# Loading x in four strided pieces, spaced over the score sets, instead of one 1 MB transfer

## The reference

```python
B, F, E = 2048, 200, 64                       # r_feature (B, F, E), weight (F, E, E), float32
bilinear = einsum('bie,ied->bid', feature, weight)
out      = einsum('bid,bjd->bij', bilinear, feature)   # (2048, 200, 200)
```

## Time and profile before

| what | value |
|---|---|
| median of 3 runs | 1367.65 us (1362.97 to 1375.2) |
| the profiled execution's own time | 1377.25 us, its span 1375.5 us |
| PE busy | 1213.2 us (88%) |
| DVE, ACT, POOL busy | 1028.0, 1042.1 and 375.3 us |
| bytes moved by DMA | 439.68 MB, mean 320 GB/s |

### The profile page before, as it was taken

The page is one execution under the profiler, slowest core; times in us unless marked ns, Lnnn a source line. Parts: engine busy times, 40 slices in busy tenths (PEclk is TensorE's granted clock), DMA queues, the critical chain, the costliest instruction groups (busy, mean ns, idle before and its releaser), DMA issues.

```text
span 1375.5 us, 57357 instructions
## 1 busy us (share of the span) xinstructions
PE 1213.2 (88%) x24384; PEld 1032.7 (75%) x24384; DVE 1028.0 (75%) x2308; ACT 1042.1 (76%) x1297; POOL 375.3 (27%) x647
## 2 busy tenths in 40 slices
PE   5998998989889898998989989898898988988986
PEld 5787777877779777887778967787677886777853
DVE  1577886777778777787778867787777776777996
ACT  4877887877778776787877968777787877877964
POOL 2222222322223222232222322222232232222322
PEclk8999999999999999999999999999999999999999
DMA  9698998989989899898989989899898998989888
GB/s 259 198 354 315 351 323 316 335 299 335 332 314 350 290 334 352 298 337 303 361 322 332 334 288 349 317 340 320 310 342 301 334 338 286 327 309 342 311 322 310
DMA packets 163821, 439.68 MB, mean 320 GB/s; under 512 B 49904, under 2 KB 49904, under 8 KB 151280
## 3 DMA queue, kind: packets, MB, share of 16 engines
q1 hardware_dynamic: 123632, 317.90, 61.1%
q0 software_dynamic: 39936, 118.12, 28.2%
HBM read 108.13 MB, written 327.68 MB: 317 GB/s over the span
## 4 chain that ended last, share of the span: by engine, by line
PE 54%; DMA 20%; DVE 9%; ACT 6%; issue 6%; SPq 3%; ACTq 0%; POOLq 0%; POOL 0%
PE ps L372 36%; DMA out_dram<-staging 19%; PE ps L340 10%; PE ps L355 9%; ACT staging L401 4%; DVE staging L401 3%; SPq L270 3%; DVE win L452 3%; ACT bl L423 2%; DMA x<-feature_dram 2%; DVE win L459 2%; DVE win L460 1%; DVE win L451 1%; ACT xt L411 0%; ACTq L400 0%
## 5 line engine op out<-in xcount | busy, mean ns | idle before, releaser
L372 PE MATMUL ps<-win,bl 64*64 64x200 f32 x16384 | 848.8, 341 | 87.5 <-ACT staging L401 45.4
L401 ACT COPY staging<-ps 128x800 f32<-128x800 f32 x768 | 613.3, 858 | 264.1 <-PE ps L372 108.0
L372 PEld LDWEIGHTS ps<-win,bl 64*64 64x64 f32 x16384 | 670.6, 177 | 187.5 <-issue 93.6
L313 POOL DMA_DIRECT2D out_dram<-staging x512 | 293.4, 577 | 915.7 <-DVE staging L401 607.4
L401 DVE COPY staging<-ps 128x800 f32<-128x800 f32 x256 | 253.1, 988 | 221.0 <-PE ps L372 220.4
L423 ACT COPY bl<-ps 128x1024 f32<-128x1024 f32 (+2 forms) x320 | 285.2, 920 | 16.0 <-PE ps L355 15.9
L452 DVE COPY win<-xt 128x400 f32<-128x400 f32 x512 | 290.0, 566 | 6.9
L355 PE MATMUL ps<-xt,w 64*64 64x128 f32 x6400 | 248.0, 278 | 46.6 <-ACT staging L401 26.8
L355 PEld LDWEIGHTS ps<-xt,w 64*64 64x64 f32 x6400 | 204.7, 135 | 73.6 <-issue 67.0
L411 ACT COPY xt<-ps 128x1024 f32<-128x1024 f32 (+1 forms) x208 | 211.9, 1019 | 43.2 <-PE ps L340 41.8
L340 PE MATMUL ps<-ident,x 128*128 128x128 f32 x1600 | 227.2, 286 | 18.5 <-DMA x<-feature_dram 14.5
(11 more groups left out here) (4 smaller groups left out, 0.4 us busy)
## 6 DMA issues: line engine op xcount, KB each, us to landing
out_dram<-staging SPq DMA_DIRECT2D x768, 400.0 KB, 5.9
x<-feature_dram POOLq DMA_DIRECT2D x96, 1024.0 KB, 9.5
out_dram<-staging POOLq DMA_DIRECT2D x512, 25.0 KB, 5.0
x<-feature_dram POOLq DMA_DIRECT2D x16, 224.0 KB, 5.9
w<-weight_dram SPq DMA_DIRECT2D x12, 256.0 KB, 11.0
x<-feature_dram POOLq DMA_DIRECT2D x16, 32.0 KB, 5.6
w<-weight_dram SPq DMA_DIRECT2D x1, 64.0 KB, 5.8
w<-weight_dram SPq DMA_DIRECT2D x1, 48.0 KB, 4.5
```

Source lines behind the costliest of these rows:

```text
L313: nc.gpsimd.dma_start(out_v[98 * g:98 * g + 2, OCT * q:OCT * q + OCT, :], staging[64 * g + SPARE[0]:64 * g + SPARE[1] + 1:4, slot].rearran ...
L372: last = nc.tensor.matmul(tile[64 * g:64 * g + 64, r, at:at + F], rows_of_bl(n, r, g, i, s), win[64 * r:64 * r + 64, q % WSLOTS, 2 * (s % ...
L401: copy(staging[:, slot, s % OCT], tile_of("s", n, s)[:, :, 0:2 * F]).then_inc(staged, 1)
```

## The change

Each 1 MB load becomes four of 256 KB. Piece k takes the partitions k, k + 4, k + 8, ... (32 of them, 8 KB each). In the steady state the pieces of one load are assigned to positions in POOL's program that are two sets apart: the first stands one set behind the one at which the 1 MB load stood, the others at 3, 5 and 7 sets behind it. For the load that becomes free with u = 12 (set 51) all four stand another four sets later (56, 58, 60, 62). Every piece has the same wait on `transposed` ahead of it as the load had, and PE waits for all four pieces of a slot. The 224 KB and 32 KB loads stay whole. Ahead of the first block the four pieces of a load follow each other directly.

```diff
+    PIECES = 4
+    APART = 2
...
+    def pieces_of_load(at):
+        return PIECES if at % NX < NX - 1 else 1
...
+    loads_after = defaultdict(list)
+    for n in range(BLOCKS):
+        for s, u in transposed_at.items():
+            at = (n + 1) * NX + u // 2 + XSLOTS
+            if (u % 2 or u == NG - 1) and at < BLOCKS * NX:
+                for piece in range(pieces_of_load(at)):
+                    loads_after[n * SETS + s + 1 + 2 * APART * (u == NG - 1) + APART * piece].append((at, piece))
...
-            def load_x(at):
+            def load_x(at, piece):
...
-                nc.gpsimd.dma_start(x[:, at % XSLOTS, 0:size], rows[:, first + E:first + E + size]
+                batches = slice(piece, NB, pieces_of_load(at))
+                nc.gpsimd.dma_start(x[batches, at % XSLOTS, 0:size], rows[batches, first + E:first + E + size]
                                     ).then_inc(x_loaded[at % XSLOTS], 16)
...
-                    if s in transposed_at and (transposed_at[s] % 2 or transposed_at[s] == NG - 1):
-                        at = (n + 1) * NX + transposed_at[s] // 2 + XSLOTS
-                        if at < BLOCKS * NX:
-                            load_x(at)
+            for s in range(BLOCKS * SETS):
+                if (s + 1) % OCT == 0:
+                    store_rest(s // OCT)
+                for at, piece in loads_after[s]:
+                    load_x(at, piece)
...
-                pe.wait_ge(x_loaded[at % XSLOTS], 16 * (at // XSLOTS + 1))
+                pe.wait_ge(x_loaded[at % XSLOTS], 16 * sum(map(pieces_of_load, range(at % XSLOTS, at + 1, XSLOTS))))
```

More of the change, by code:

```diff
@@ L1 @@
+from collections import defaultdict
 from contextlib import ExitStack
@@ L296, in load_x @@
                     nc.gpsimd.dma_start(x[:, at % XSLOTS, size:size + E], rows[:, 0:E]).then_inc(wrap_loaded, 16)
-            for u in range(XSLOTS):
-                load_x(u)
+            for at in range(XSLOTS):
+                for piece in range(pieces_of_load(at)):
+                    load_x(at, piece)
             nc.gpsimd.memset(ident[:], 0.0).then_inc(ident_zero, 1)
@@ L316, in store_rest @@
                                         ).then_inc(rest_written[slot], 16)
[L318 to L323, removed]
-                    if s in transposed_at and (transposed_at[s] % 2 or transposed_at[s] == NG - 1):
-                        at = (n + 1) * NX + transposed_at[s] // 2 + XSLOTS
-                        if at < BLOCKS * NX:
-                            load_x(at)
+            for at in range(XSLOTS, NX + XSLOTS):
+                for piece in range(pieces_of_load(at)):
+                    load_x(at, piece)
+            for s in range(BLOCKS * SETS):
+                if (s + 1) % OCT == 0:
+                    store_rest(s // OCT)
+                for at, piece in loads_after[s]:
+                    load_x(at, piece)
         @block.tensor
```

## The result

The changed kernel takes 1442.69 us (median of four runs, 1431.02 to 1453.36), the kernel before 1369.39 us in the runs beside it: a ratio of 1.051, 95% interval 1.042 to 1.060. It is slower, as forecast, but by 73 us and not by 27.

The account below looks back on a forecast made before the run. No engine was full; late output stores made ACT wait 104.1 us for staging slots. Block end -45, middle +69 and start +3 sum to +27 us: 1395 us from a median of 1367.65, range 1315 to 1445.

Parts of the forecast that it names:

- The end of the block: Loads behind groups 11 and 12 spread over groups 11 to 14: set 60's wait shrinks, -45 us over 14 blocks.
- Rival C: Block end: pieces hold group 12's stores as long as whole loads, so no gain there; 1440 us, chance 0.08.
- Ahead of the first block: Before the first block each load's last piece is issued 1.7 us later: 0 to 5 us, taken as +3 us.
- The place of the last piece: Mid-block: last piece, behind rest stores, makes PE wait 6.28 us a block at u = 4, 6, 8, 10; net +69 us.
- rival A: Mid-block pieces land quickly, so the kernel is faster: 1343 us at 5.0 us landing, 1311 at 4.0; chance 0.32.
- The sign named for this term: Mid-block: PE's total wait for loads of x rises from 14.5 us to 70 to 95 us, most at u = 4.
- Not all of it is new time: Behind u = 4, 6 and 8, stores catch up while PE waits; staging-slot waits fall away, returning 1.68 us a block.

Follow-up runs that it names:

- e2: Changed kernel, but only the two loads at the end of a block are split and spaced, all others whole and where they were: 1320.04 us, 0.963 of the kernel before.
- e5: Changed kernel plus sixteen identity transposes on PE ahead of the wait for x at u = 4, 6 and 8: 1405.21 us, 1.028 of the kernel before.

## Why the prediction was right and wrong

**The end of the block: right.** -45 us was forecast, -49.6 measured, and e2 shows it alone with -50.9 in the block ends. The mechanism is the one forecast: in the 14 blocks the third store of group 12 lands in 7.9 us on average (11.2 before, 8.0 taken), and ACT idles 2.0 us before set 60 (4.7 before, 2.1 forecast). Rival C, that the end keeps its wait, did not happen.

**Ahead of the first block: right**, +3 forecast, +2.9 measured.

**The place of the last piece: right, its price a little too high.** PE waits at u = 4, 6, 8 and 10 for a piece that POOL issues behind the rest stores of groups 2, 4, 6 and 8. The price of the waits was 6.28 us a block, 94 in all, and is 5.06, 76 in all: a piece landed in 5.7 us and not 5.9, and POOL issued it 0.57 us behind the second rest store and not 0.82 (in block 4 the two rest stores take from 429.30 to 430.45, and the pieces begin at 430.44, half of that behind the second). With 6.38, 6.21 and 6.30 us after that store at u = 4, 6 and 8 the piece came close to the 6.27 at which rival A was to take over: with 76 us in place of 94 the forecast's sum is +9 us, within one per cent. The sign named for this term was off: PE's wait for x was to rise to the order of 70 to 95 us, which is the lengthening of the path, and rose to 152.6, since the new wait also took the place of other idle time and of slower matmuls in the same stretches.

**The step that failed** is the one that began "Not all of it is new time". The slot waits behind u = 4, 6 and 8 did fall away as it says: at full clock, in e5, the stretches add up to 188.2 us, 22.7 less than before, where 15 x 1.68 = 25 was forecast. But it priced PE's work behind a wait at the clock it had before the wait, and so put the clock at nothing without a reason. 26 of 45 times the clock was lower, and 22.7 us of gain became 19.3 us of loss: 42 us that the sum did not have. They make the difference between the forecast of 27 and the 54 us of the profiled execution: 42 from the clock, 2.5 from slot waits that came back a little less, less 18 by which the waits were smaller and 4.6 by which the end gained more, and the 5 us between the stretches. Without the 42 us the parts come to 12 us, less than one per cent: most of the slowdown came from a term that the forecast did not have, and in so far its sign is luck. Some of the loss stays without the falls, as e5 shows, which has its own transposes to pay and is 2.8% above the kernel before.

The Trainium skill (TensorE: Matmul & The Clock Gate, "HAM oscillation — how this bites in real kernels") tells of a kernel in which each DMA wait lets the clock fall and the work after the wait starts slowly, again at every tile. The traces agree in part: the clock was lower in 26 of 45 stretches, with rows at 0.56 to 0.74, and stayed full in the other 19. The kernel before had its own sign of it: at the end of block 0, where set 60 waits, the stretch from set 48 to the next set 0 stands at a granted clock of 0.86, and at the end of block 14, where it doesn't, at 1.00. The row of block 0:

```profile
110.48:133.24 22.76, 18.38 (x398) 16.63 (x397) 15.87 (x37) 16.64 (x23) 5.83 (x10) 0.86 0.93 337
```

That sign had no visible price there: eleven of the 14 block ends with loads stand at 0.85 to 0.94 and take 22.05 to 23.86 us, and the three at 1.00 take as long, 22.72 to 23.53. Behind u = 4, 6 and 8 it had one, since PE was busy all through those stretches.

**The measured difference of 73 us** is more than the profile's 54, because the changed kernel's profiled execution was the fastest of its runs, with the highest clock, and the kernel before's was slower than its median.

## What to carry to other kernels

Before a transfer is split and its parts are moved later, take the time between the last part's real issue and its use from the trace; where the issuing engine waits for something else in between, the part's place in the program is that of the wait ahead of it, not the position written in the code. Where the rest of the kernel waits for PE, a new wait on PE is to be priced twice, once as idle time and once as slower work behind it; in e5, which keeps PE busy while it waits, most of the second price was gone. When two changes go together, try each alone: here one gained 50 us and the other lost over 100, and a distance of one set instead of two kept the gain of the first and lost nothing.

## What was not expected of the hardware

Sixteen additional transposes ahead of a wait made the changed kernel 34 us faster, though they compute nothing of use: behind 44 of the 45 waits the granted clock stayed at full. And four DMAs of 256 KB issued one behind the other beside heavy stores made a faster kernel than one of 1 MB, 1349.55 against 1368.28 us, with nothing else changed; why stays open.
